# Attention stage: the last batch's norm is computed inside the first loop iteration instead of in the layout before it

## The reference

```python
h = _layernorm(x) * (1 + ca) + sa
x = x + ga * _L1_attn_ref(h, ...)     # the part this change touches
h = _layernorm(x) * (1 + cb) + sb
x = x + gb * _L1_ffn_ref(h, ...)      # experts, two of eight per token
```

```python
q = rms_norm(x, qn_scale) @ q_w.T + q_b ; k likewise ; v = x @ v_w.T + v_b
weights = sigmoid(q k^T / 4);  weights = weights / (sum(weights) + eps)
attn = weights @ v;  return attn @ o_w.T + o_b
```

## Time and profile before

| | us |
|---|---|
| median of 3 runs | 1613.15 |
| lowest, highest | 1610.79, 1613.45 |
| the profiled execution | 1611.74 |
| its span in the profile | 1610.0 |

### The profile page before, as it was taken

The page is one execution under the profiler, slowest core; times in us unless marked ns, Lnnn a source line. Parts: engine busy times, 40 slices in busy tenths (PEclk is TensorE's granted clock), DMA queues, the critical chain, the costliest instruction groups (busy, mean ns, idle before and its releaser), DMA issues. The chain is left out here.

```text
span 1610.0 us, 29263 instructions
## 1 busy us (share of the span) xinstructions
PE 1464.9 (91%) x10406; PEld 1172.9 (73%) x10406; DVE 1140.0 (71%) x2334; ACT 929.5 (58%) x1172; POOL 417.0 (26%) x413
## 2 busy tenths in 40 slices
PE   6899999868999977899999999866999999999998
PEld 4788888757888875355545544446889999999987
DVE  4677777568878875665786686455568787877768
ACT  2566665434555534776776676743347777777752
POOL 1122322330001012232153344223213333333320
PEclk9899999989999987999999999987999999999999
DMA  7000000210000000120000000005038888888864
GB/s 275 1 1 0 0 0 0 79 42 1 0 0 0 0 27 1 70 91 1 2 29 12 22 25 22 18 18 195 28 103 231 231 234 235 231 236 232 235 157 157
DMA packets 65455, 130.51 MB, mean 81 GB/s; under 512 B 8249, under 2 KB 38754, under 8 KB 64866
## 3 DMA queue, kind: packets, MB, share of 16 engines
q1 hardware_dynamic: 51074, 110.37, 22.1%
q0 software_dynamic: 14304, 19.15, 5.7%
HBM read 97.50 MB, written 32.00 MB: 80 GB/s over the span
## 5 line engine op out<-in xcount | busy, mean ns | idle before, releaser
L1822 ACT ACTIVATE at_wide<-at_sc_ps 128x2048 f32<-128x2048 f32 x128 | 240.6, 1879 | 117.3 <-PE at_sc_ps L1658 116.1
L2276 POOL DMA_INDIRECT sums<-e_y,e_row_ids x78 | 121.6, 1559 | 247.8 <-ACT e_y L2431 235.9
L52 PE MATMUL e_gate_ps<-e_h_parts,e_w 128*128 128x256 f32 (+1 forms) x1128 | 176.9, 304 | 7.0 <-DVE e_w L2485 3.4
L2485 DVE TENSOR_TENSOR e_w<-e_raw,e_w 128x1024 fp32r<-128x1024 f32 x123 | 147.1, 1222 | 42.7 <-ACT e_w L2384 42.7
L52 PE MATMUL e_up_ps<-e_h_parts,e_w 128*128 128x256 f32 (+1 forms) x1128 | 175.0, 302 | 0.0
L52 PEld LDWEIGHTS e_gate_ps<-e_h_parts,e_w 128*128 128x128 f32 x1128 | 155.3, 193 | 14.7 <-DVE e_w L2485 3.5
L52 PEld LDWEIGHTS e_up_ps<-e_h_parts,e_w 128*128 128x128 f32 x1128 | 155.2, 193 | 7.9
L1672 PE MATMUL at_o_ps<-at_wide,at_v_ones 128*32 128x512 f32 x1024 | 142.5, 630 | 0.0
L2341 PE MATMUL e_down_ps<-e_w,e_hidden 128*128 128x256 f32 x936 | 127.9, 286 | 1.0 <-DVE e_hidden L2534 1.0
L2384 ACT ACTIVATE e_w<-e_raw 128x1024 fp32r<-128x1024 f32 x123 | 125.3, 1048 | 6.1 <-DMA e_raw<-in_experts 6.1
L1658 PE MATMUL at_sc_ps<-at_qT,at_kT 32*128 32x512 f32 x1024 | 96.3, 450 | 28.9 <-ACT at_wide L1822 26.9
(11 more groups left out here) (351 smaller groups left out, 2735.2 us busy)
## 6 DMA issues: line engine op xcount, KB each, us to landing
e_raw<-in_experts SPq DMA_DIRECT2D x123, 512.0 KB
e_rows_in<-slots SPq DMA_DIRECT2D x39, 272.0 KB
sums<-shared SPq DMA_DIRECT2D x17, 256.0 KB
x<-in_L_attn_x SPq DMA_DIRECT2D x8, 512.0 KB, 9.4
gate<-gates SPq DMA_DIRECT2D x4, 1024.0 KB
slots<-shared SPq DMA_DIRECT2D x15, 272.0 KB
out<-x SPq DMA_DIRECT2D x7, 512.0 KB, 3.1
e_sums<-sums SPq DMA_DIRECT2D x4, 512.0 KB, 4.4
```

The lines of the kernel that those rows point to most:

```text
L52: last = pe.matmul(out, left(i), right(j), start=n == 0, stop=n == len(steps) - 1)
L1822: nc.scalar.activation(wide[:, u % 2, :], sc_ps[:].rearrange("p n s -> p (n s)"), ACT.Sigmoid, scale=float(HD) ** -0.5).then_inc(sig_done, 1)
L2276: pool.indirect_dma_start(c.sums_dram[:, :], bass.IndirectOffsetOnAxis(ap=row_ids[:, j % 2, t:t + 1], axis=0), y[:, j % 2, t, :], None, co ...
L2485: nc.vector.tensor_tensor(w[:, buf, REST, q], raw[:, q], w[:, buf, HEAD, q].bitcast(F32), ALU.subtract).then_inc(w_split, 1)
```

## The change

The last batch's norm leaves the layout and takes the empty slots of iteration 0 and of the start of iteration 1. VectorE's statistics come between the residuals of tiles 0 and 1 of batch 1, its normalising between those of tiles 2 and 3, now written to `c.hT_store[:, 7]` by token. TensorE transposes at unit 14 into `a_ps`, after a wait for all residuals of batch 1 (these are read from `a_ps`). `modulate_last` is split by feature chunk: one after the sigmoid of unit 15 of iteration 0, one after that of unit 0 of iteration 1. The sums of squares follow `attend` of unit 0 of iteration 1, and VectorE evicts them as the first thing of iteration 1. `values(2, ...)` waits for that eviction (`last_kept`), since it writes the same banks. GpSimd's power moves to iteration 1, its inversion between the cosines of tiles 1 and 2. The squares lie in `twice_own` instead of `wide`.

Apart from that, VectorE's order in the layout is changed: the residuals of tile 0 and the addition of tile 2 come before the rotation of tile 3; the residuals of tile 1 stay ahead of the fourth addition.

```diff
--- before.py
+++ after.py
@@ -1426,8 +1426,7 @@
         denom, inv_denom = sb("denom", [P, 2, NT * QUAD]), sb("inv_denom", [P, 2, NT * QUAD])
         o_parts = sb("o_parts", [P, 2, KC, S], F32R)
         gate_bias = sb("gate_bias", [P, D])
-        xn_last = wide[:, 0, 0:NT * D].rearrange("p (t d) -> p t d", d=D)
-        last_squares = wide[:, 1, 0:KC * S].rearrange("p (k s) -> p k s", k=KC)
+        last_squares = twice_own[:].rearrange("p (k s) -> p k s", k=KC)
         a_ps = c.psum("at_a_ps", 2, ctx)
         sc_ps = c.psum("at_sc_ps", QUAD, ctx)
         o_ps = c.psum("at_o_ps", 2, ctx)
@@ -1557,8 +1556,14 @@
                     if past:
                         bias_x(b - 1)
                     scatter(b, 2, 7)
+                    if b == 1:
+                        pool.wait_ge(last_kept, 1)
+                        nc.gpsimd.tensor_tensor(c.inv_rms[:, B - 1], c.mean_square[:, B - 1], c.neg_half[:, 0:NT], ALU.pow
+                                                ).then_inc(last_kept, 1)
                     if past:
                         norm.invert(pool, b - 1)
+                    else:
+                        norm_last.invert(pool, 0)
                     scatter(b, 3, 8)
                     scatter(b, 4, 10)
                     if coming:
@@ -1573,7 +1578,6 @@
                 pool.memset(ones[:], 1.0)
                 pool.memset(v_ones[:], 1.0).then_inc(tables_set, 1)
                 pool.wait_ge(tables_set, 1)
-                norm_last.invert(pool, 0)
                 pool.memset(sign[:], 1.0)
                 pool.memset(odd[:], 1.0).then_inc(strips_set, 1)
                 pool.wait_ge(strips_set, 1)
@@ -1586,9 +1590,6 @@
                 place_values(0, 0, early=True)
                 for t in range(NT):
                     times_cos(0, t)
-                pool.wait_ge(last_kept, 1)
-                nc.gpsimd.tensor_tensor(c.inv_rms[:, B - 1], c.mean_square[:, B - 1], c.neg_half[:, 0:NT], ALU.pow
-                                        ).then_inc(last_kept, 1)
                 iteration(0, 0, False, True, early=True)
                 ds.set_tables(pool)
                 for b in range(1, B):
@@ -1600,6 +1601,8 @@
             def _(pe):
                 def values(b, *ts):
                     for t in ts:
+                        if b == 2 and t in (0, 2):
+                            pe.wait_ge(last_kept, 1)
                         if t == 0:
                             pe.wait_ge(h_split, b + 1)
                             if b >= 3:
@@ -1712,6 +1715,21 @@
                                                     router_w[:, k, :], start=k == 0, stop=k == KC - 1)
                     last.then_inc(logits_done, 1)
 
+                def last_by_feature():
+                    pe.wait_ge(qT_kept, NT * 2)
+                    pe.wait_ge(kT_kept, NT * 2)
+                    pe.wait_ge(last_rows_done, 1)
+                    transposes(nc.tensor, c, a_ps, rows_by_token(B - 1)).then_inc(last_turned, 1)
+
+                def sum_last_squares():
+                    pe.wait_ge(last_h_done, KC)
+                    pe.wait_ge(tables_set, 1)
+                    for t in range(NT):
+                        for k in range(KC):
+                            last = nc.tensor.matmul(a_ps[:, 1, t:t + 1], last_squares[:, k, t * P:(t + 1) * P], ones[:],
+                                                    start=k == 0, stop=k == KC - 1)
+                    last.then_inc(last_squares_done, 1)
+
                 def iteration(b, par, past, coming):
 
                     for u in range(UNITS):
@@ -1729,6 +1747,10 @@
                         attend(b, par, u)
                         if u % NT == 1 and u > NT:
                             quad_by_token(b, u // NT - 1)
+                        if u == 14 and not past:
+                            last_by_feature()
+                        if u == 0 and b == 1:
+                            sum_last_squares()
                         if past:
                             if u == 1:
                                 quad_by_token(b - 1, QUADS - 1)
@@ -1770,28 +1792,18 @@
 
                 values(0, 0, 1)
                 values(0, 2, 3)
-                pe.wait_ge(last_rows_done, 1)
-                transposes(nc.tensor, c, o_ps, xn_last).then_inc(last_turned, 1)
                 for t in range(NT):
                     queries_keys(0, t)
                 by_feature(0, 0, 0)
                 by_feature(0, 0, 1)
                 by_feature(0, 1, 0)
                 by_feature(0, 1, 1)
-                pe.wait_ge(last_h_done, 1)
-                pe.wait_ge(tables_set, 1)
-                for t in range(NT):
-                    for k in range(KC):
-                        last = nc.tensor.matmul(o_ps[:, 0, t:t + 1], last_squares[:, k, t * P:(t + 1) * P], ones[:],
-                                                start=k == 0, stop=k == KC - 1)
-                last.then_inc(last_squares_done, 1)
                 by_feature(0, 2, 0)
                 by_feature(0, 2, 1)
                 by_feature(0, 3, 0)
                 by_feature(0, 3, 1)
                 scores(0, 0, 0)
                 pe.wait_ge(tables_loaded, N_TABLES)
-                pe.wait_ge(last_kept, 1)
                 for b in range(B):
                     iteration(b, b % 2, b > 0, b < B - 1)
                 ds.make_rows(pe, B - 3, 1, sc_ps[:, 0, :])
@@ -1846,9 +1858,20 @@
                     if KC - 1 in ks:
                         last.then_inc(next_done, 1)
 
+                def modulate_last(k):
+                    act.wait_ge(last_turned, 1)
+                    shift, scale = c.mod[:, 1, SA, k, B - 1:B], c.mod[:, 1, CA, k, B - 1:B]
+                    nc.scalar.activation(c.hT[:, k, B - 1, :], a_ps[:, k, :], ACT.Identity, bias=shift, scale=scale)
+                    nc.scalar.activation(last_squares[:, k, :], a_ps[:, k, :], ACT.Square, bias=shift,
+                                         scale=scale).then_inc(last_h_done, 1)
+
                 def iteration(b, par, past, coming, h_after=True):
                     for u in range(UNITS):
                         sigmoids(b, u)
+                        if u == 15 and not past:
+                            modulate_last(0)
+                        if u == 0 and b == 1:
+                            modulate_last(1)
                         if past and u == 5:
                             output_head(b - 1)
                         if coming and u in (9, 10, 13, 14):
@@ -1865,17 +1888,8 @@
                             act.wait_ge(logits_kept, b - 1)
                             ds.probabilities(act, b - 2)
 
-                def modulate_last():
-                    act.wait_ge(last_turned, 1)
-                    for k in range(KC):
-                        shift, scale = c.mod[:, 1, SA, k, B - 1:B], c.mod[:, 1, CA, k, B - 1:B]
-                        nc.scalar.activation(c.hT[:, k, B - 1, :], o_ps[:, k, :], ACT.Identity, bias=shift, scale=scale)
-                        last = nc.scalar.activation(last_squares[:, k, :], o_ps[:, k, :], ACT.Square, bias=shift, scale=scale)
-                    last.then_inc(last_h_done, 1)
-
                 head_of_h(0)
                 nc.scalar.activation(spare[:], c.neg_half[:, 0:1], ACT.Sigmoid)
-                modulate_last()
                 act.wait_ge(strips_set, 2)
                 for t in range(NT):
                     heads_by_feature(0, t)
@@ -2011,6 +2025,10 @@
 
                 def iteration(b, par, past, coming, h_after=True):
                     n, p = b + 1, b - 1
+                    if b == 1:
+                        dve.wait_ge(last_squares_done, 1)
+                        nc.vector.tensor_scalar(c.mean_square[:, B - 1], a_ps[:, 1, 0:NT], 1.0 / D, RMS_EPS, ALU.mult,
+                                                ALU.add).then_inc(last_kept, 1)
                     if past:
                         keep_quad(p, QUADS - 1)
                     if b >= 2:
@@ -2041,6 +2059,9 @@
                         keep_by_feature(n, 0)
                     if past:
                         moments(p)
+                    else:
+                        norm_last.gather(lambda t: c.x[:, B - 1, t, :])
+                        norm_last.aggregate(dve, 0)
                     if coming:
                         keep_by_feature(n, 1)
                     divide_quad(b, 1)
@@ -2054,6 +2075,8 @@
                         keep_by_feature(n, 2)
                     if past:
                         normalise(p)
+                    else:
+                        norm_last.apply(dve, 0, rows_by_token(B - 1), lambda t: c.x[:, B - 1, t, :], last_rows_done)
                     if coming:
                         keep_by_feature(n, 3)
                     if b >= 2:
@@ -2065,10 +2088,7 @@
                         keep_logits(p)
                         ds.place_tokens(dve, b - 2, ranks)
 
-                norm_last.gather(lambda t: c.x[:, B - 1, t, :])
-                norm_last.aggregate(dve, 0)
```

(8 more changed lines are left out.)

## The result

The changed kernel takes 1603.28 us (median of 16 runs, 1600.99 to 1609.8), the kernel before beside it 1611.86 (16 runs, 1608.04 to 1613.93). The ratio of the two is 0.9955 with a 95% interval of 0.9943 to 0.9966, which is 7.3 us faster; the medians themselves lie 8.6 us apart. The forecast was 1614.4, within 1611.2 to 1617.2.

A forecast was written before the change was run, and what follows sets the result against it. It saw engine hand-overs bounding the layout and TensorE and ScalarE alternating in the loop. Terms -2.1 + 0.1 + 1.0 + 2.1 + 1.5 = +2.6 on 1611.74 gave 1614.4 us, range 1611.2 to 1617.2.

The forecast's parts named there:

- Start of the layout, 0.7: Attention layout's start: without the statistics, the residual of h and the first values start 0.7 us earlier.
- Transposes gone, 0.8: TensorE in the layout: removing the last batch's eight transposes before the first queries and keys saves 0.8 us.
- clock back early: Rival, chance 0.08: TensorE's clock is back at 1.00 by the first scores, saving 3.5 us, total 1609.3 us.
- VectorE's order, 0.6: Layout's tail: with tile 2 transposed earlier, fourth addition to scores takes 3.6 us instead of 4.16, gaining 0.6.
- 0.1 for the moments: Iteration 0: VectorE's moments between the residuals of tiles 0 and 1 of the next batch cost 0.1 us.
- 1.0 at the boundary: Iterations 0 to 1: `modulate_last(0)` ahead of the next sigmoid on ScalarE makes that sigmoid 1.0 us later.
- the 2.1 forecast: Iteration 1, TensorE: 16 one-column sums (1.84 us) and the values' wait on `last_kept` (0.3) add 2.1 us.
- The clock, +1.5: Iteration 1: TensorE's clock falls at the new sums, lengthening the value product by 1.24 and scores by 0.27 us.
- high clock holds: Rival, chance 0.23: the clock stays high through iteration 1's new sums, so +1.1 us in all, 1612.8 us.

The follow-up runs named there:

- after_again: The changed kernel run and profiled once more without an edit: median 1604.21 us, ratio 0.9960 to the kernel before.
- the late routing: Routing block of iterations 2 to 7 moved behind unit 0's attention product: kernel before 1611.53 us (0.9984), changed kernel 1609.48 us (0.9985), ratios to the unedited kernel before.

## Why the prediction was wrong

Step by step, against the traces:

- Start of the layout, 0.7: values 2.37 us after the head of h begins, before 3.05: 0.7, right. Transposes gone, 0.8: right. But at the scaling of tile 0 the gain was 2.15 (603.73 - 595.30 against 605.19 - 594.61) and not 1.5, the value products taking 4.55 us for the 24 instead of 5.15, with more of them at the high clock. That was luck of this execution: they took 5.28 in `after_again`. The first unit step of iteration 0 that holds a value product took 4.47 instead of 5.66 (4.89 in `after_again`), as that low stretch ended earlier. So the rival "clock back early" came true in part, for about 1 us and not 3.5: the first scores took 1.23 us as before, which is the low clock.
- VectorE's order, 0.6, with no new wait: from the end of the fourth addition to the scores 3.59 instead of 4.16, right; tile 3's first head waits where forecast.
- Iteration 0: 0.1 for the moments, measured nothing (units 10 to 12 took 9.17 against 9.16). 1.0 at the boundary: 3.85 instead of 2.87, right.
- Iteration 1: the second `modulate_last` made the step to unit 1 0.2 longer (3.08 instead of 2.87), and the sums and the wait made the next one 2.0 longer (5.27 instead of 3.28). Together that is 2.2 for the 2.1 forecast, scores to scores: right.
- **The clock, +1.5: this is the step that failed, twice.** It let the clock fall at the new sums; in all six profiles of kernels with these sums the step is 5.26 to 5.28: it never fell. And, far more, it kept the six falls that were there at the price of the one trace: the sum has no term for the clock of iterations 2 to 7, since the prediction read only the 90 us that the change touches. Their price is what moved, by 4.9 us in the mean of two profiles each: 47.7 and 48.0 us in the kernel before, 46.0 and 39.9 in the changed one. No rival of the prediction had it. The "high clock holds" rival (1612.8) is right about the sums and still 9 us above the median.

The work sums to about nothing, as forecast for the high clock (+1.1): up to the sigmoid of unit 2 of iteration 1, behind which the change adds only a small GpSimd operation and a repeated wait for the same eviction, it is +0.5 in the mean of nine profiles. Two comparisons of the two kernels under one edit agree with that: with the late routing 0.9985 to 0.9984, with the padding 0.9937 to 0.9933. Their intervals (0.1 to 0.2% to either side of each) exclude 7 us; whether the work is 1 us more or none they can't tell. With two additions in both the sign even turns over, which no amount of work explains.

What is shown: useless work in the layout shortens the kernel before by 6.7 us and lengthens the changed one by about 4, the same work behind the loop does neither, and shorter runs are those with a higher mean clock. The six steps carry most of what the profiles differ by (rest 1561.9 to 1567.7 over all profiles, their sum 35.9 to 49.3), and the length of each goes with its low stretch. The profiled pairs of both kernels differ by 5.5 in the mean, of which 4.9 are in these steps.

What is argued: that the time of entry into the loop sets the moments of the falls. The layout of the kernel before took anything from 33.3 to 34.15 us without an edit, and yet its runs stayed within 1608 to 1617. What stays open: the changed kernel's shortest runs (1601) have no profile, so that their six steps are inferred from the mean clock; why the kernel before meets the same pattern in most runs; and what makes the clock fall, the narrow matmuls or the idle gap ahead of them. What the clock did in the stage before, which puts the start of the attention stage anywhere from 593.8 to 596.6, was not varied.

The Trainium skill (TensorE: Matmul & The Clock Gate, Part 1) says that the moment at which the clock changes is not tied to the program's start and differs from run to run. The traces agree as far as the changed kernel's two profiles go (46.0 and 39.9 us in the same six steps); the two of the kernel before (47.7 and 48.0) do not show it. The Trainium skill advises in the same part not to fit the rise of the clock to the high level in a model, as its penalty is under 1% of a typical kernel's span. That is so here too, but a gain of 0.45% of the time was the thing to be explained, and 4.9 of the 5.5 us between the profiled pairs lie in steps with low stretches.

## What to carry to other kernels

Where a profile shows a clock below full speed at a repeated place, a small change far ahead of that place can bring or cost more there than its own work. Before crediting a change, put a useless delay of the same size in its position, and compare the two versions once more under a second edit. One trace is one pattern: when the runs of a kernel scatter by more than the effect, take two profiles, and hold the time of every run against its mean clock. Then work on the place itself: padding the narrow matmuls to 64 columns went with 12 us less in both kernels and cost 0.05 us a block.

## What the runs showed of the hardware

- Sixteen matmuls of 8 columns take 1.95 us at the high clock, of 64 columns 2.00 us, of one column 1.84 and 1.95, each with a weight load of 128 columns. So the number of columns hardly counts up to 64. Where the clock fell among the eight-column ones they took up to 3.05 us, and a set of one-column matmuls at the low clock in the layout took 3.41.
- A fall in the routing block cost 1.4 to 1.6 us (6.54 against 5.17 in iteration 2, 7.62 to 7.72 against 6.11 in iterations 3 to 6) when the low stretch lasted 3.4 us, and 3.1 to 3.2 us (8.24, 9.18 to 9.29) when it lasted 6.8 us and still covered the products behind the block.
- Sums of one column behind the attention product did not lower the clock in any of six profiles, nor did the eight-column ones always: 5.17 to 5.18 at the start of iteration 2 in seven profiles with the unedited block.
